# The head of a linear-attention phase: one signal and one buffer for each weight, and another order of loads and splits

## The reference

```python
qkv = x @ Wqkv + bqkv                      # 256 -> 3 x 256, 16 heads of 16
xn = x / jnp.maximum(jnp.linalg.norm(x, axis=-1, keepdims=True), 1e-12)   # q and k, by head
proj = jnp.einsum('bhtd,rhdm->rbhtm', xn, omega)
arg = jnp.clip(proj * sqrt_2s - s, -20.0, 20.0)      # s: the nodes
feat = jnp.exp(arg) / np.sqrt(M) * sqrt(weights)
...                                        # causal sums over chunks of 128
return out @ Wout + bout
x = _layernorm(x + attention(x))
```

## Time and profile before

| | us |
|---|---|
| median of 3 runs | 1658.53 (1656.6 to 1659.21) |
| the profiled execution | 1657.14 |
| its span, first to last instruction | 1655.5 |
| TensorE busy (matmul) | 1415.1 (85%) |
| VectorE busy | 934.4 (56%) |
| ScalarE busy | 679.9 (41%) |
| GpSimd busy | 509.5 (31%) |
| mean granted clock of TensorE | 0.917 |

### The profile page before, as it was taken

The page is one execution under the profiler, slowest core; times in us unless marked ns, Lnnn a source line. Parts: engine busy times, 40 slices in busy tenths (PEclk is TensorE's granted clock), DMA queues, the critical chain, the costliest instruction groups (busy, mean ns, idle before and its releaser), DMA issues. The chain is left out here.

```text
span 1655.5 us, 34268 instructions
## 1 busy us (share of the span) xinstructions
PE 1415.1 (85%) x12248; PEld 1219.7 (74%) x12248; DVE 934.4 (56%) x2089; ACT 679.9 (41%) x1252; POOL 509.5 (31%) x395
## 2 busy tenths in 40 slices
PE   6799999717998897987988489999997999999980
PEld 5687878605666675665766388888886999999970
DVE  4866665435767657666676425543434555555545
ACT  2456566412434343343433233222223555555541
POOL 0234433301243332333410000643302444444440
PEclk9799999957999899899989699999998999999995
DMA  6234321030032131322200630424218888888866
GB/s 240 80 122 136 134 83 46 13 132 13 2 128 75 65 114 38 127 76 70 82 26 27 225 148 26 142 90 150 68 51 210 235 232 239 237 230 238 240 141 203
DMA packets 107783, 204.25 MB, mean 123 GB/s; under 512 B 18496, under 2 KB 81344, under 8 KB 101440
## 3 DMA queue, kind: packets, MB, share of 16 engines
q1 hardware_dynamic: 79248, 143.88, 26.7%
q0 software_dynamic: 23088, 54.31, 11.4%
q10 hardware_dynamic: 5376, 5.13, 0.9%
HBM read 144.72 MB, written 58.55 MB: 123 GB/s over the span
## 5 line engine op out<-in xcount | busy, mean ns | idle before, releaser
L2080 PE MATMUL e_ps<-e_xhl,e_whl 128*128 128x256 f32 x1872 | 249.3, 283 | 3.6 <-DMA e_whl<-wlo 3.5
L2080 PEld LDWEIGHTS e_ps<-e_xhl,e_whl 128*128 128x128 f32 x1872 | 234.0, 190 | 4.1 <-issue 4.1
L1669 PE MATMUL d_ps<-d_xhl,d_whl 128*128 128x512 f32 x768 | 192.0, 399 | 5.4 <-DVE d_whl L1740 5.4
L1669 PEld LDWEIGHTS d_ps<-d_xhl,d_whl 128*128 128x128 f32 x768 | 143.3, 192 | 34.5 <-issue 5.7
L1977 POOL DMA_INDIRECT xs<-e_y,e_slot_id x78 | 121.5, 1558 | 83.0 <-ACT e_y L2007 68.1
L1215 ACT ACTIVATE c_qf<-c_cf,c_fc 128x512 f32<-128x512 f32 x64 | 46.1, 721 | 229.7 <-DVE c_cf L1337 229.7
L2060 PE MATMUL e_ps<-e_whl,e_ghl 128*128 128x256 f32 x936 | 137.7, 283 | 0.5 <-DVE e_ghl L2155 0.5
L345 POOL TENSOR_TENSOR b_hhl<-b_h,b_hhl 128x512 fp32r<-128x512 f32 x64 | 85.5, 1339 | 157.3 <-ACT b_hhl L572 125.1
L2143 DVE TENSOR_TENSOR e_g<-e_ps,e_act_h 128x256 f32<-128x256 f32 x156 | 66.3, 425 | 115.6 <-ACT e_act_h L2021 115.5
L2060 PEld LDWEIGHTS e_ps<-e_whl,e_ghl 128*128 128x128 f32 x936 | 120.5, 188 | 0.7 <-ACT e_ghl L2031 0.7
L1844 DVE TENSOR_TENSOR d_g<-d_ps,d_act_h 128x512 f32<-128x512 f32 x64 | 44.3, 692 | 123.8 <-PE d_ps L1669 89.5
(11 more groups left out here) (307 smaller groups left out, 2667.5 us busy)
## 6 DMA issues: line engine op xcount, KB each, us to landing
e_whl<-wlo SPq DMA_DIRECT2D x39, 1024.0 KB, 5.0
e_whl<-wlo SPq DMA_DIRECT2D x39, 512.0 KB
c_eraw<-in_expert_w POOLq DMA_DIRECT2D x24, 512.0 KB, 4.7
wlo<-c_elo POOLq DMA_DIRECT2D x24, 512.0 KB, 3.0
wall<-in_expert_w SPq DMA_DIRECT2D x8, 1536.0 KB, 8.2
xg<-b_zeros POOLq DMA_DIRECT2D x13, 780.0 KB, 4.3
e_xr<-xg SPq DMA_DIRECT2D x39, 260.0 KB, 3.6
b_xts<-in_x_t SPq DMA_DIRECT2D x14, 512.0 KB, 5.4
```

Of the source, the lines that this page charges most:

```text
L1669: mm = pe.matmul(ps[:, H + 2 * (m % 2) + w, :], whl[:, wp, e, lo:lo + P], xhl[:, k, xp, kd, :], start=q == 0, stop=q == 3 * KD - 1)
L2080: mm = pe.matmul(ps[:, H + m, w * SLOT:(w + 1) * SLOT], whl[:, k, wp, lo:lo + P], xhl[:, k, xp, kd, :], start=q == 0, stop=q == 3 * KD - 1)
```

## The change

Each weight gets a signal (`ids_in`, `bias_in`, `nodes_in`, `omega_in`, `wout_in`), and wout and omega are loaded into buffers that nothing uses before step 1 (`out` and `z`), so that no load waits. The order of loads becomes wqkv, x, identity, qkv bias, nodes (three loads), omega, mask, wout, output bias, residual. TensorE starts its transposes once the identity and x are there, and waits for wqkv's low part before FQ(0) and for all low parts before the first features. ScalarE and VectorE split wqkv first; VectorE then does the small steps on the nodes (`node_scales`), and inside `body(-1)`, behind the evacuations of FT(1), FQ(0), FQ(1) and FQ(3), the roots, omega's scaling, the query bias and the low parts of wout and omega. ScalarE does the logarithm and the high parts of wout and omega after its copy for FT(1).

```diff
@@ -889,7 +889,9 @@
         PAIRS_ALL = PAIRS * STEPS
-        WEIGHTS = 16 * 7
+        WEIGHTS = 16 * 2
+        omr = z[:].rearrange("p b d -> p (b d)")
+        wor = out[:].rearrange("p b d -> p (b d)")[:, 0:KD * D]
@@ -906,6 +908,9 @@
+        def first(i):
+            return isinstance(i, int) and i == -1
@@ -970,16 +975,16 @@
             sp.dma_start(raw[:], wqkv.rearrange("p k n -> p (k n)")).then_inc(s["raw_in"], 16)
-            sp.dma_start(nw[:, 0:1], nodes).then_inc(s["weights_in"], 16)
-            sp.dma_start(nw[:, 1:2], weights).then_inc(s["weights_in"], 16)
-            for dst, src in ((ns[:, 0], nodes.rearrange("p o -> (p o)").partition_broadcast(P)), (ids[:], ident), (tri[:], masks[0]),
-                             (bq[:], bqkv.partition_broadcast(P)), (bo[:], bout.partition_broadcast(P))):
-                sp.dma_start(dst, src).then_inc(s["weights_in"], 16)
             sp.dma_start(xr[:], x2[0]).then_inc(s["x_in"], 16)
-            sp.wait_ge(s["raw_lo"], 1)
-            sp.dma_start(raw[:, 0:KD * D], wout.rearrange("p k n -> p (k n)")).then_inc(s["raw_in"], 16)
-            sp.wait_ge(s["raw_lo"], 2)
-            sp.dma_start(raw[:, 0:PAIRS * P], omega.rearrange("p k n -> p (k n)")).then_inc(s["raw_in"], 16)
+            sp.dma_start(ids[:], ident).then_inc(s["ids_in"], 16)
+            sp.dma_start(bq[:], bqkv.partition_broadcast(P)).then_inc(s["bias_in"], 16)
+            sp.dma_start(ns[:, 0], nodes.rearrange("p o -> (p o)").partition_broadcast(P)).then_inc(s["nodes_in"], 16)
+            sp.dma_start(nw[:, 0:1], nodes).then_inc(s["nodes_in"], 16)
+            sp.dma_start(nw[:, 1:2], weights).then_inc(s["nodes_in"], 16)
+            sp.dma_start(omr, omega.rearrange("p k n -> p (k n)")).then_inc(s["omega_in"], 16)
+            sp.dma_start(tri[:], masks[0]).then_inc(s["weights_in"], 16)
+            sp.dma_start(wor, wout.rearrange("p k n -> p (k n)")).then_inc(s["wout_in"], 16)
+            sp.dma_start(bo[:], bout.partition_broadcast(P)).then_inc(s["weights_in"], 16)
@@ -1045,9 +1050,9 @@
                 gp.dma_start(eraw[:, k], ew[:, k * EC:(k + 1) * EC]).then_inc(eraw_in[k], 16)
-            gp.wait_ge(s["weights_in"], WEIGHTS)
...
             body(0)
+            gp.wait_ge(s["weights_in"], WEIGHTS)
@@ -1081,6 +1086,8 @@
                 elif name == "FQ":
+                    if first(i) and a == 0:
+                        pe.wait_ge(s["raw_lo"], 1)
@@ -1117,6 +1124,8 @@
                 wait(pe, "clip_done", n)
+                if isinstance(i, int) and i == 0 and t == 0:
+                    pe.wait_ge(s["raw_lo"], 4)
@@ -1180,25 +1189,24 @@
-            pe.wait_ge(s["weights_in"], WEIGHTS)
-            pe.wait_ge(s["raw_lo"], 4)
-            pe.wait_ge(s["fc_ready"], 2)
+            pe.wait_ge(s["ids_in"], 16)
...
         def _(act):
-            def high(dst, n):
-                act.activation(dst, raw[:, 0:n], ACT.Copy).then_inc(s["raw_hi"], 1)
-            act.wait_ge(s["fc_ready"], 1)
-            act.activation(fc[:, LNA], fc[:, QBIAS], ACT.Ln).then_inc(s["raw_hi"], 1)
+            def high(dst, src):
+                act.activation(dst, src, ACT.Copy).then_inc(s["raw_hi"], 1)
+            def other_weights():
+                act.wait_ge(s["fc_ready"], 1)
+                act.activation(fc[:, LNA], fc[:, QBIAS], ACT.Ln).then_inc(s["ln_done"], 1)
+                act.wait_ge(s["wout_in"], 16)
+                high(wo[:, 0].rearrange("p k n -> p (k n)"), wor)
+                act.wait_ge(s["raw_lo"], 2)
+                high(om[:, 0].rearrange("p k n -> p (k n)"), omr)
             act.wait_ge(s["raw_in"], 16)
-            high(wq[:, 0].rearrange("p k n -> p (k n)"), KD * 3 * D)
-            act.wait_ge(s["raw_in"], 32)
-            high(wo[:, 0].rearrange("p k n -> p (k n)"), KD * D)
-            act.wait_ge(s["raw_lo"], 3)
-            high(om[:, 0].rearrange("p k n -> p (k n)"), PAIRS * P)
-            act.wait_ge(s["fc_ready"], 2)
+            high(wq[:, 0].rearrange("p k n -> p (k n)"), raw[:])
@@ -1240,6 +1248,8 @@
                 for t in range(PAIRS):
+                    if isinstance(i, int) and i == 0 and t == 0:
+                        act.wait_ge(s["fc_ready"], 2)
@@ -1249,6 +1259,8 @@
                     x_high(i, t, C_)
+                    if first(i) and t == 2:
+                        other_weights()
@@ -1262,34 +1274,43 @@
             pre.mark(ve.memset(va[:, :, :, HD:HD + 1], 1.0))
-            ve.wait_ge(s["weights_in"], WEIGHTS)
-            pre.link(ve.tensor_scalar(ns[:, 1], ns[:, 0], 0.0, 2.0, ALU.max, ALU.mult))
-            rsqrt(pre, ns[:, 1], ns[:, 2], ns[:, 3], nsi[:])
-            pre.link(ve.tensor_tensor(ns[:, 1], ns[:, 1], ns[:, 2], ALU.mult))
-            pre.mark(ve.tensor_scalar(fc[:, HIGH], nw[:, 0:1], 20.0, None, ALU.add))
-            pre.mark(ve.tensor_scalar(fc[:, LOW], nw[:, 0:1], -20.0, None, ALU.add))
-            pre.mark(ve.tensor_scalar(fc[:, KBIAS], nw[:, 0:1], -1.0, None, ALU.mult))
-            pre.link(ve.tensor_scalar(fc[:, AMP], nw[:, 1:2], 0.0, 1.0 / MF, ALU.max, ALU.mult))
-            ve.tensor_scalar(fc[:, QBIAS], fc[:, AMP], TINY, None, ALU.max).then_inc(s["fc_ready"], 1)
-            pre.link(ve.tensor_scalar(fc[:, NONE], fc[:, AMP], TINY, -1e30, ALU.is_lt, ALU.mult))
+            def low(dst, src, hi):
+                ve.tensor_tensor(dst, src, hi.bitcast(F32), ALU.subtract).then_inc(s["raw_lo"], 1)
+            def node_scales():
+                ve.wait_ge(s["nodes_in"], 48)
+                pre.mark(ve.tensor_scalar(fc[:, HIGH], nw[:, 0:1], 20.0, None, ALU.add))
+                pre.mark(ve.tensor_scalar(fc[:, LOW], nw[:, 0:1], -20.0, None, ALU.add))
+                pre.mark(ve.tensor_scalar(fc[:, KBIAS], nw[:, 0:1], -1.0, None, ALU.mult))
+                pre.link(ve.tensor_scalar(fc[:, AMP], nw[:, 1:2], 0.0, 1.0 / MF, ALU.max, ALU.mult))
+                ve.tensor_scalar(fc[:, QBIAS], fc[:, AMP], TINY, None, ALU.max).then_inc(s["fc_ready"], 1)
+                pre.link(ve.tensor_scalar(fc[:, NONE], fc[:, AMP], TINY, -1e30, ALU.is_lt, ALU.mult))
+                pre.link(ve.tensor_scalar(ns[:, 1], ns[:, 0], 0.0, 2.0, ALU.max, ALU.mult))
+            def node_roots():
+                rsqrt(pre, ns[:, 1], ns[:, 2], ns[:, 3], nsi[:])
+                pre.link(ve.tensor_tensor(ns[:, 1], ns[:, 1], ns[:, 2], ALU.mult))
+            def scale_omega():
+                ve.wait_ge(s["omega_in"], 16)
+                scaled = omr.rearrange("p (k n) -> p k n", k=PAIRS)
+                ve.tensor_tensor(scaled, scaled, ns[:, 1].unsqueeze(1).to_broadcast([P, PAIRS, P]), ALU.mult).then_inc(s["raw_lo"], 1)
+            def query_bias():
+                ve.wait_ge(s["ln_done"], 1)
+                pre.link(ve.tensor_tensor(fc[:, QBIAS], fc[:, LNA], fc[:, KBIAS], ALU.add))
+                ve.tensor_tensor(fc[:, QBIAS], fc[:, QBIAS], fc[:, NONE], ALU.add).then_inc(s["fc_ready"], 1)
+            def other_weights():
+                ve.wait_ge(s["raw_hi"], 2)
+                low(wo[:, 1].rearrange("p k n -> p (k n)"), wor, wo[:, 0].rearrange("p k n -> p (k n)"))
+                ve.wait_ge(s["raw_hi"], 3)
+                low(om[:, 1].rearrange("p k n -> p (k n)"), omr, om[:, 0].rearrange("p k n -> p (k n)"))
             ve.wait_ge(s["raw_hi"], 1)
-            pre.link(ve.tensor_tensor(fc[:, QBIAS], fc[:, LNA], fc[:, KBIAS], ALU.add))
-            ve.tensor_tensor(fc[:, QBIAS], fc[:, QBIAS], fc[:, NONE], ALU.add).then_inc(s["fc_ready"], 1)
-            def low(dst, hi, n):
-                ve.tensor_tensor(dst, raw[:, 0:n], hi.bitcast(F32), ALU.subtract).then_inc(s["raw_lo"], 1)
-            ve.wait_ge(s["raw_hi"], 2)
-            low(wq[:, 1].rearrange("p k n -> p (k n)"), wq[:, 0].rearrange("p k n -> p (k n)"), KD * 3 * D)
-            ve.wait_ge(s["raw_hi"], 3)
-            low(wo[:, 1].rearrange("p k n -> p (k n)"), wo[:, 0].rearrange("p k n -> p (k n)"), KD * D)
-            ve.wait_ge(s["raw_in"], 48)
-            scaled = raw[:, 0:PAIRS * P].rearrange("p (k n) -> p k n", k=PAIRS)
-            ve.tensor_tensor(scaled, scaled, ns[:, 1].unsqueeze(1).to_broadcast([P, PAIRS, P]), ALU.mult).then_inc(s["raw_lo"], 1)
-            ve.wait_ge(s["raw_hi"], 4)
-            low(om[:, 1].rearrange("p k n -> p (k n)"), om[:, 0].rearrange("p k n -> p (k n)"), PAIRS * P)
+            low(wq[:, 1].rearrange("p k n -> p (k n)"), raw[:], wq[:, 0].rearrange("p k n -> p (k n)"))
+            node_scales()
@@ -1329,6 +1350,16 @@
                     ins.then_inc(s["x_free"], 1)
+                    if first(i):
+                        if (name, a) == ("FT", 1):
+                            node_roots()
+                            ve.wait_ge(s["bias_in"], 16)
+                        if (name, a) == ("FQ", 0):
+                            scale_omega()
+                        if (name, a) == ("FQ", 1):
+                            query_bias()
+                        if (name, a) == ("FQ", 3):
```

(5 more changed lines are left out.)

## The result

| | before | changed |
|---|---|---|
| median, us | 1658.53 (1656.2 to 1659.21, 5 runs) | 1646.91 (1643.18 to 1648.77, 5 runs) |
| ratio | | 0.993, 95% interval 0.9913 to 0.9948 |
| profiled execution, us | 1657.14 (span 1655.5) | 1644.69 (span 1643.1) |

The kernel is faster by 11.6 us (0.7%), where 19 was forecast, and 1646.91 lies 0.9 us above the range that was given for 8 in 10 (1634 to 1646), 4.4 above the forecast's own ends (1636 to 1642.5). A third comparison with fresh runs gave 0.9933 (0.9916 to 0.995) again; a second one, on a chip where the kernel before is 23 us slower and the changed one 17, 0.9887 (0.9861 to 0.9913).

A forecast was written before the change was run, and what follows sets the result against it. The attention phase's head was bound by a chain of loads, waits and small VectorE steps. FQ(0) 21.0 us sooner, less 2.1 for interleaved work, saves 18.9 from 1657.14: 1638.2, forecast 1639 (1636 to 1642.5; 8 in 10: 1634 to 1646).

The forecast's parts named there:

- F: Start of the first projection, FQ(0): from 369.38 to 348.4, 21.0 us sooner (19.6 to 22.8); wrong if after 350.
- the rest to the end: Sign: from the norm chain to the end, 1274.4 us, the same within 3 us, or the prediction is wrong.
- The first transpose: Head: transposes of x start once x and identity land behind GpSimd's loads, at 344.2 (343.2 to 345.1).
- The wait for the nodes: VectorE before FQ(0): nodes land at 346.0, with 0.6 for two 4-byte loads; ends last, by 0.85 us.
- VectorE's work between the evacuations: From FQ(0) to the norm chain: added steps lengthen 11.7 to 13.8 us, costing 2.1 (1.9 to 3.6).
- GpSimd's second squaring, just covered: Before the norm chain: the squaring ends at F + 11.3, VectorE's low parts at F + 11.35.
- Three waits that are long fulfilled … moved, not altered: After FQ(0): waits raw_lo 4, fc_ready 2 and weights_in cost nothing; everything from the norm chain on only moves.
- Rival (b), the granted clock: Loop: low-clock stretches fall elsewhere, 5.9 us each; more give 1645 to 1648 (chance 0.09), one fewer 1633 (0.08).
- Rival (a): Head: loads come in a block, nodes land at 349.5, FQ(0) at 352, 15.3 us saved: 1643; chance 0.10.
- (c): Loop: slower, more than 3.2 further stretches at clock 0.80 turn the gain over; five give 1668; chance 0.03.
- (d): Head: FQ(0) is released as late as before, for instance by omega's low part: 1657; chance 0.02.
- The reading that the projections might all run at the lower clock: Projections: waits idling TensorE put it back to the lower clock; 3.6 us in place of 2.1, sum 1639.7.

The follow-up runs named there:

- scales_behind: Changed kernel with VectorE's wait for the nodes and the small steps behind it moved after FT(1)'s evacuation; ratio 0.991 to the kernel before.
- table_early: Changed kernel with ScalarE's wait for the query bias moved two slots before the copies of normalised q and k; ratio 0.9862 to the kernel before.
- best1: Changed kernel with nodes' loads first, node steps, roots and query bias before FT(0)'s evacuation, other steps where GpSimd idles, ScalarE's wait moved; ratio 0.9837 to kernel before.
- best2: `best1` with GpSimd's two loads of expert weights issued only when the identity is there; ratio 0.9815 to the kernel before, 0.989 (1638.52 us) when repeated.

## Why the prediction was wrong

The cause was right: the waits at the head went, and the norm chain came 15.4 us sooner. Three terms of the sum failed, and two of the signs of being wrong that the prediction named came true: the norm chain began 15.76 us after F (over 15.4), and the rest to the end took 1279.0 us where 1274.4 were given, 4.6 more. The third did not, but only just: F is 14.78, or 349.97 on the scale of before, and 350 was the limit.

A row of the kernel before that the second point rests on (KB, us from issue to landing):

```profile
c_nw<-in_weights SPq DMA_DIRECT2D x1, 0.5 KB, 6.1
```

- **The first transpose** (9.01 forecast in the phase, 9.02 measured; 9.35 and 9.38 in the other two traces): a load released it, as forecast, but the agreement to 0.01 us is luck. wqkv landed at 4.3, not 4.8. GpSimd's second load landed at 9.3; the forecast had both through at 7.4, since it took the median of the two, 6.7 in rows 3, for the end of both. x landed at 7.5, before it, and the identity, 64 KB, 1.5 us behind x, where the forecast gives it 0.2.
- **The wait for the nodes** ends last, as the prediction said, but its term was mis-sized: 10.8 forecast, 12.56 measured. The row broadcast of the nodes landed at 335.85 + 8.3 = 344.15 or 10.6 in the phase, 0.4 after the forecast's 10.2; the two 4-byte loads behind it took 1.9 us together, not 0.6. The step that took one such load's landing behind wqkv in the kernel before as the price of two was too low. The same trace had the better one: the second 4-byte load (the row above) was issued at 336.07, so it landed at 342.2, 1.6 behind the first. `scales_behind` shows that this wait, with its small steps, held FQ(0). F moved by 19.4 in place of 21.0; cost 1.6 us.
- **VectorE's work between the evacuations**: the order was right and each evacuation came when forecast (FQ(0)'s ended at F + 5.1, FQ(1)'s at F + 6.9; 5.25 and 7.2 forecast) until GpSimd's first squaring began. The step that failed is the adding of durations of operations as if they ran alone: query bias 0.4, omega's low part 1.23. The first took 2.0, the second 2.91 with its wait. Of the first's 1.6 us only 0.6 went on, since FQ(3) ran meanwhile (its evacuation ended at F + 10.0 in place of 9.4); by the end of omega's low part it was 2.1 (F + 13.5 in place of 11.35). "GpSimd's second squaring, just covered" looked at GpSimd's results only, not at what its running does to VectorE. Term: 4.0 in place of 2.1, and outside its own ends (1.9 to 3.6); cost 1.9 us.
- **"Three waits that are long fulfilled … moved, not altered"**: wrong for one. The wait was fulfilled, but with it two waits stood before the first exponential, and the clip's came to stand on the table load. Cost 1.2 us by the state's first matmul (1.34 at the exponential), and `table_early` takes it back.
- **Rival (b), the granted clock**, was given 0.09 upwards, at 5.9 us for a stretch. In the profiled execution it took 3.9 us, behind the head. The other terms leave 18.9 - 1.6 - 1.9 - 1.2 = 14.2 us, or 1644.3 from the median of before. The median, 1646.91, is 2.6 above that. This isn't explained: the ratio's interval allows 8.6 to 14.4 us saved, so it may be the runs' own spread, of which the clock's stretches are a part; only executions with a trace show them.
- **Rival (a)**, loads in a block: no; up to the nodes the loads landed in the queue's order. **(c)** and **(d)**: no. The reading that the projections might all run at the lower clock, with 3.6 in place of 2.1: no, the last two ran at 1.00, and the 4.0 has another cause.

What stays open: why the ratio was lower on the slower chip (0.9887, with 14.7 us saved by the state's first matmul there, too), and why, from the shared experts' first matmul to the routed experts' first one, it takes 334 to 348 us on the slower chips against 320 to 324; both kernels have it (341.0 and 320.5 before, 347.8 and 320.4 in the changed kernel).

## What to carry to other kernels

When a step is put beside other engines' work, price it with what runs then: a VectorE operation with two tensors in SBUF costs up to the whole length of the GpSimd operation beside it (0.15 us became 1.89), and a scalar operand or an operand in PSUM avoids that. A wait that never waits still takes a place: look whether it pushes another wait onto a table load. And price small loads by how far behind the load ahead they land with the same traffic beside them, not by their bytes.

## What the runs showed of the hardware that I had not expected

- Two-operand VectorE work in SBUF and GpSimd work exclude each other per instruction: 0.15 us became 1.89, 1.23 became 2.91, GpSimd's 1.89 became 2.27.
- A 512-byte load of 128 pieces of 4 bytes landed 0.5 and 1.4 us behind the load ahead of it (344.15, 344.64 and 346.07 in the changed kernel); first in the queue, 2.1 and 1.6 us beside GpSimd's loads (`best1`), 0.7 and 0.6 without them (`best2`).
- The same program has, behind the same head, one stretch of 3.41 or of 13.65 us at the lower granted clock, worth 3.8 us (66.7 against 70.5). Another stretch of it differs by 3.3 us from one execution to the next (320.4 and 323.8).
